# Early-fusion block on one core: attention written out, image outputs around the last softmax, slot maps shared by DVE and ACT

## What is computed

```python
x  = tokens(img, txt)                       # patch embedding, two layer norms, positions
x  = x + scan_mixer(layernorm(x))           # layer 0, a selective scan of 16 states
x  = x + moe0(x)                            # 4 groups x 2 experts of 512, one group per token
q, k, v = norm(x) @ Wq.T, norm(x) @ Wk.T, norm(x) @ Wv.T     # layer 1, q and k with rotary positions
x  = x + softmax(causal(q @ k.T / 16)) @ v @ Wf.T + bf
lg = layernorm(x) @ wr + br                 # 4 experts of 1024, the best two per token
for e in top2(lg): x += gate[e] * (gelu(norm(x) @ w1[e] + b1[e]) @ w2[e] + b2[e])
```

## Time and profile before

| | |
|---|---|
| median of 3 runs | 855.33 us (855.31 to 856.13) |
| profiled execution | 856.54 us, of which the span of instructions is 854.7 us |
| mean granted TensorE clock | 0.935 |
| busy in the span | PE 756.7 us, DVE 507.6, ACT 357.6, POOL 354.1 |
| first product of the layer-0 experts | 146.5 us |
| end of ACT's normalising before them | 133.9 us |
| attention batches | about 378 to 520.8 us |
| image outputs, statistics | to 542.7 us |
| logits, gates, positions | to 559.1 us |
| slot map, first gathers | to 585.0 us |
| layer-1 experts | to 839 us, output to 854.7 |

### The profile page before, as it was taken

The page is one execution under the profiler, slowest core; times in us unless marked ns, Lnnn a source line. Parts: engine busy times, 40 slices in busy tenths (PEclk is TensorE's granted clock), DMA queues, the critical chain, the costliest instruction groups (busy, mean ns, idle before and its releaser), DMA issues.

```text
span 854.7 us, 17322 instructions
## 1 busy us (share of the span) xinstructions
PE 756.7 (89%) x5428; PEld 592.4 (69%) x5429; DVE 507.6 (59%) x1265; ACT 357.6 (42%) x803; POOL 354.1 (41%) x308
## 2 busy tenths in 40 slices
PE   3998932999999999959999999967999999999991
PEld 2767921666666666647777776755888888888871
DVE  4896989433333343349887877795555555555550
ACT  5795663333333333324534333503433334443440
POOL 2449951123232232214556653002455555555431
PEclk9996975999999999969999997987999999999996
DMA  9950044142112121152121210521133333333234
GB/s 264 415 232 2 1 136 155 19 107 33 28 25 37 25 34 27 16 155 90 51 74 50 71 52 29 185 85 51 33 49 49 50 49 49 49 49 49 32 40 139
DMA packets 37174, 65.98 MB, mean 77 GB/s; under 512 B 3776, under 2 KB 29360, under 8 KB 35568
## 3 DMA queue, kind: packets, MB, share of 16 engines
q1 hardware_dynamic: 23696, 46.90, 16.3%
q0 software_dynamic: 13248, 18.21, 13.4%
q10 hardware_dynamic: 192, 0.38, 0.1%
HBM read 44.83 MB, written 23.35 MB: 80 GB/s over the span
## 4 chain that ended last, share of the span: by engine, by line
PE 75%; DVE 15%; ACT 4%; DMA 2%; issue 2%; POOLq 0%; SPq 0%; POOL 0%; DVEq 0%
PE PS L762 15%; PE PS L955 14%; PE PS L968 14%; PE PS L780 7%; PE PS L1299 5%; PE PS L770 2%; PE PS L1340 2%; PE PS L1295 2%; PE PS L1330 2%; PE PS L1332 2%; DVE tops L709 2%; PE PS L1312 1%; PE PS L1303 1%; DMA Y<-in_wtok_dram 1%; PE PS L940 1%
## 5 line engine op out<-in xcount | busy, mean ns | idle before, releaser
L762 PE MATMUL PS<-X,Y 128*128 x576 | 134.7, 384 | 1.3 <-DVE Y L860 1.3
L1125 POOL DMA_INDIRECT sum<-X,dest x45 | 88.4, 1965 | 97.2 <-ACT X L1036 81.9
L968 PE MATMUL PS<-X 128*128 x720 | 125.8, 273 | 1.9 <-ACT X L1036 1.9
L955 PE MATMUL PS<-X 128*128 128x256 f16 (+1 forms) x768 | 124.7, 268 | 2.2 <-DVE X L1056 1.5
L1026 ACT ACTIVATE X<-PS,X 128x256 f32<-128x256 f32 (+1 forms) x192 | 72.8, 463 | 105.8 <-PE PS L955 102.6
L871 DVE SCALAR_TENSOR_TENSOR Y<-PS,Y 128x512 f32<-128x512 f32 x48 | 36.0, 751 | 112.2 <-PE PS L762 112.2
L955 PE MATMUL PS<-X,Y 128*128 128x256 f16 (+1 forms) x384 | 101.1, 267 | 0.0
L926 POOL DMA_INDIRECT sum<-Y,dest x24 | 38.1, 1586 | 148.2 <-ACT Y L837 148.2
L762 PEld LDWEIGHTS PS<-X,Y 128*128 128x128 f16 x576 | 57.0, 99 | 60.8 <-issue 4.3
L968 PE MATMUL PS<-Y,X 128*128 x360 | 98.2, 273 | 0.0
L955 PEld LDWEIGHTS PS<-X 128*128 x768 | 72.3, 98 | 12.8 <-issue 3.0
(11 more groups left out here) (378 smaller groups left out, 1475.8 us busy)
## 6 DMA issues: line engine op xcount, KB each, us to landing
X<-in_w_dram SPq DMA_DIRECT2D x11, 1024.0 KB, 16.1
stage<-in_w_dram SPq DMA_DIRECT2D x16, 512.0 KB, 3.3
sum<-h SPq DMA_DIRECT2D x2, 2048.0 KB, 7.6
xs<-Y SPq DMA_DIRECT2D x2, 1040.0 KB, 5.1
xs<-Y SPq DMA_DIRECT2D x2, 1032.0 KB, 5.5
h<-in_txt_dram SPq DMA_DIRECT2D x2, 1024.0 KB, 17.9
Y<-in_patches_dram SPq DMA_DIRECT2D x3, 672.0 KB, 8.8
sum<-h SPq DMA_DIRECT2D x2, 768.0 KB, 4.0
```

The costliest lines, as they stand in the source:

```text
L762: ins = nc.tensor.matmul(PS[:, 2 * u + s, 0:F0], x_[:, slot, k, :], w_[:, at_:at_ + F0], start=(n == 0), stop=(n == 3 * KC - 1))
L955: ins = nc.tensor.matmul(PS[:, 2 * s + c // 2, (c % 2) * T1:(c % 2) * T1 + tokens], part[:, off:off + P], x_[:, slot, k, 0:tokens], start= ...
L968: ins = nc.tensor.matmul(PS[:, 4 + a, 0:D], h_[:, s, c, a * P:(a + 1) * P], part[:, off:off + D], start=(s == 0 and c == 0 and n == 0), st ...
L1125: nc.gpsimd.indirect_dma_start(out=sum1, out_offset=bass.IndirectOffsetOnAxis(ap=dest[:, i:i + 1], axis=0), in_=y1buf[:, u % 2, i - first_ ...
```

## The change

- All 16 batches are written out on PE, ACT and DVE. `IMAGE_BIAS` = 8 lets the image biases on GpSimd start in batch 8 instead of 6.
- `base_images` goes. Behind the text output of batches 4 to 9 PE makes the base of one image tile in the same bank; DVE scales it in `add_text`. Std (`newt`) is made once at the end of batch 3.
- In batch 15 PE makes image outputs 0, 1 and 2 instead of `base_images`, then transposes, text output 14, values 15, image output 3, text output 15, image outputs 4 and 5. The banks are now 0, 1, 2, 7, 3, 4. DVE adds in a matching order; moments of 14 text tiles are in between.
- Maxima of layer-1 weights are taken in halves of 1,024 (`top_of_half`) in batches 4, 5, 6, 7, 10, 11 and 14, the eighth between the logits and the gates.
- In `positions` the comparisons read integers directly; `minus` is the negated row number; ACT makes the first 6 (layer 0) or 12 (layer 1) token columns of `inrow` as relu(1 - |iota - row|), DVE the others in two or three pieces. Four operations for `source` become one; constants for this (`slot_at`, a repeated `k_tile`) are made on GpSimd at the start.
- The bias products of experts 0 and 1 start once image tile 0 is added. ACT copies both banks of `biases_out` away. The sum is made in parts: experts 0 and 1 and b2 before the slot map, expert 2 behind it, expert 3 behind the transposes of unit 0 (`meanwhile`). The subtraction for `rest1` moves into DVE's unit 0.

```diff
+ACT_ROWS = (6, 12)
+PIECES = (2, 3)
...
+        def act_rows(act, done, inrow):
+            act.wait_ge(rows_known, done + 1)
+            n = ACT_ROWS[done]
+            column = minus.rearrange("p c t -> p (c t)")
+            for c in range(n):
+                nc.scalar.activation(nearly[:, c, :], k_iota, ACT.Abs, bias=column[:, c:c + 1]).then_inc(act_hot, 1)
+            act.wait_ge(act_hot, sum(ACT_ROWS[0:done + 1]) + done)
+            nc.scalar.activation(inrow[:, 0:n, :], nearly[:, 0:n, :], ACT.Relu, bias=1.0, scale=-1.0).then_inc(act_hot, 1)
...
             chain.link(nc.vector.tensor_copy(pos[:, 0:choices, :], slots_of))
-            chain.link(nc.vector.tensor_scalar(low7[:, 0:choices, :], pos[:, 0:choices, :], P - 1, None, ALU.bitwise_and))
-            chain.link(nc.vector.tensor_scalar(high7[:, 0:choices, :], pos[:, 0:choices, :], 7, None,
-                                               ALU.logical_shift_right))
+            chain.link(nc.vector.tensor_scalar(row_of, pos[:, 0:choices, :], P - 1, None, ALU.bitwise_and))
+            nc.vector.tensor_scalar(minus[:, 0:choices, :], row_of, -1.0, None, ALU.mult).then_inc(rows_known, 1)
+            chain.link(nc.vector.tensor_scalar(first_of, pos[:, 0:choices, :], -P, None, ALU.bitwise_and))
-            chain.link(nc.vector.tensor_copy(slots_of, high7[:, 0:choices, :]))
...
-            chain.link(nc.vector.tensor_copy(slots_of, low7[:, 0:choices, :]))
...
-            half = n // 2
-            for c0 in (0, half):
-                nc.vector.tensor_tensor(inrow[:, c0:c0 + half, :], each(slots_of, P)[:, c0:c0 + half],
-                                        along(k_iota, P)[:, c0:c0 + half], ALU.is_equal).then_inc(hot_ready, 1)
+            for c0, c1 in row_pieces(done):
+                nc.vector.tensor_tensor(inrow[:, c0:c1, :], each(row_of, P)[:, c0:c1],
+                                        along(k_iota, P)[:, c0:c1], ALU.is_equal).then_inc(hot_ready, 1)
...
             chain.link(nc.vector.tensor_copy(from_, row_))
-            chain.link(nc.vector.scalar_tensor_tensor(out=place, in0=tile_, scalar=float(P), in1=from_, op0=ALU.mult,
+            nc.vector.scalar_tensor_tensor(out=source[:, 0:tiles], in0=tile_, scalar=float(P), in1=from_, op0=ALU.mult,
+                                           op1=ALU.add).then_inc(source_ready, 1)
+            dve.wait_ge(source_ready, done + 1)
+            chain.link(nc.vector.scalar_tensor_tensor(out=from_, in0=tile_, scalar=float(P), in1=from_, op0=ALU.mult,
                                                       op1=ALU.add))
-            chain.link(nc.vector.tensor_scalar(from_, place, float(TOKENS), -float(TOKENS), ALU.is_ge, ALU.mult))
-            chain.link(nc.vector.tensor_tensor(from_, from_, place, ALU.add))
-            nc.vector.tensor_copy(source[:, 0:tiles], from_).then_inc(source_ready, 1)
-            dve.wait_ge(source_ready, done + 1)
...
             def out_text(b, slot):
...
+                if b in IMAGE_BASE:
+                    n = IMAGE_BASE.index(b)
+                    pe.wait_ge(xTi_copied, n + 1)
+                    for k in range(KC):
+                        ins = nc.tensor.matmul(PS[0:IROWS, 6, PAY1:PAY1 + E1], xTi[:, k, n * IROWS:(n + 1) * IROWS], wr1[:, k, :],
+                                               start=(k == 0), stop=(k == KC - 1))
...
             def batch(b, slot):
                 scores(b, slot)
-                if not known(b, BATCH - 1):
+                if b < BATCH - 1:
                     project(b + 1, 1 - slot)
                 else:
-                    base_images()
+                    pe.wait_ge(v_copied, BATCH)
+                    for n in range(3):
+                        out_image(n)
                 transpose_p(b, slot)
...
             heads(pe, batch)
+            out_image(3)
             out_text(BATCH - 1, 1)
...
+            pe.wait_ge(s_max, BATCH)
+            out_image(4)
+            out_image(5)
...
-            for b in range(START):
+            for b in range(BATCH - 1):
                 batch(b, b % 2)
...
+            maxima(BATCH - 1)
+            normalise_p(BATCH - 1, 1)
+            add_image(0)
+            add_image(1)
+            add_text(BATCH - 2, 0)
+            logit_base()
+            add_image(2)
+            dve.wait_ge(stats_ready, NT + BATCH - 2)
+            moments_text(range(BATCH - 2))
+            add_image(3)
             add_text(BATCH - 1, 1)
-            dve.wait_ge(stats_ready, NT + BATCH)
-            for t in range(BATCH):
-                ins = nc.vector.bn_aggr(mv[:, t, :], stats[:, t, 0, :])
+            add_image(4)
+            add_image(5)
...
-            pe.wait_ge(h3_added, NT)
             biases_out(2)
             pe_count(pe, 1)
-            biases_sum()
+            biases_sum(0, True, False)
+            biases_sum(1, False, False)
+            biases_rest()
             pe_slots(pe, 1, TOPK * NT, SLOT1, inrow1, intile1)
+            biases_sum(2, False, False)
             pe.wait_ge(slots_ready, 2)
             pe.wait_ge(dest_ready, 2)
-            pe.wait_ge(rest_ready, 1)
             pe_scale(pe, 1)
-            pe_experts1(pe)
+            pe.wait_ge(c_copied, 1)
+
+            def meanwhile():
+                biases_sum(3, False, True).then_inc(c_psum, 1)
+            pe_experts1(pe, meanwhile)
```

More of the change, by code:

```diff
@@ L533, in pe_count, with row_pieces @@
                 .then_inc(count_psum, 1)
+        def row_pieces(done):
+            first, last = ACT_ROWS[done], (1 + done) * NT
+            step = -(-(last - first) // PIECES[done])
+            return [(c, min(c + step, last)) for c in range(first, last, step)]
+        def act_rows(act, done, inrow):
[6 more added lines that the diff above has]
+            nc.scalar.activation(inrow[:, 0:n, :], nearly[:, 0:n, :], ACT.Relu, bias=1.0, scale=-1.0).then_inc(act_hot, 1)
         def pe_slots(pe, done, n, tiles, inrow, intile):
+            pieces = [c for c, _ in row_pieces(done)]
+            earlier = done * len(row_pieces(0))
+            pe.wait_ge(act_hot, sum(ACT_ROWS[0:done + 1]) + done + 1)
+            pe.wait_ge(hot_ready, earlier + 1)
             for i in range(n):
-                if i % (n // 2) == 0:
-                    pe.wait_ge(hot_ready, 2 * done + i // (n // 2) + 1)
+                if i in pieces:
+                    pe.wait_ge(hot_ready, earlier + pieces.index(i) + 1)
                 ins = nc.tensor.matmul(PS[:, 7, 0:3 * tiles], inrow[:, i, :], intile[:, i, :, :].rearrange("p a b -> p (a b)"),
@@ L724, in dve_scale @@
             top, scale_, un = amax[:, 2:3], hscale[:, 2 * layer:2 * layer + 1], hscale[:, 2 * layer + 1:2 * layer + 2]
-            chain.link(nc.vector.tensor_reduce(top, PS[:, 5 + layer, 0:P], AX, ALU.max))
+            chain.link(nc.vector.tensor_reduce(top, PS[:, 5 - layer, 0:P], AX, ALU.max))
             if layer == 0:
@@ L981, in tile @@
                     transpose_x(0, 0, 0)
+                    meanwhile()
                 products_in(i, 0, w_, slot)
@@ L1473, in run @@
                 chunk(b, slot, j)
-            for b in range(START):
+            for b in range(BATCH):
                 run(b, b % 2, b // 2)
-            with act.Fori(START // 2, BATCH // 2 - 1) as j:
-                run(2 * j, 0, j)
-                run(2 * j + 1, 1, j)
-            run(BATCH - 2, 0, BATCH // 2 - 1)
-            run(BATCH - 1, 1, BATCH // 2 - 1)
         def pool_attention(pool):
@@ L1657, in logit_base, with add_image @@
                 chain.link(nc.vector.tensor_tensor(raw1, raw1, old, ALU.add))
-            for b in range(START):
-                batch(b, b % 2)
-            with dve.Fori(START // 2, BATCH // 2 - 1) as j:
-                chain.begin(j - START // 2, 4)
-                batch(2 * j, 0)
-                batch(2 * j + 1, 1)
-                chain.end(BATCH // 2 - 1 - START // 2)
-            batch(BATCH - 2, 0)
-            batch(BATCH - 1, 1)
+            def add_image(n):
+                r = tile_rows(BATCH + n)
+                dve.wait_ge(bi_added, n + 1)
+                dve.wait_ge(pr_psum, PR_IMAGE[n])
+                hb = h[0:r, BATCH + n, :]
+                to = raw1[0:r, :, BATCH + n:BATCH + n + 1]
+                nc.vector.tensor_tensor(to, PS[0:r, OUT_BANK[n], D:PAY1].unsqueeze(2), to, ALU.add)
+                nc.vector.tensor_tensor(hb, PS[0:r, OUT_BANK[n], 0:D], hb, ALU.add).then_inc(h3_added, 1)
+                dve.wait_ge(h3_added, H3_IMAGE[n])
+                nc.vector.bn_stats(stats[:, BATCH + n, 0, :], h[:, BATCH + n, :]).then_inc(stats_ready, 1)
@@ L1732, in biases_out, with biases_sum @@
                 ins.then_inc(c_psum, 1)
-            def biases_sum():
+            def biases_sum(e, first, last):
+                for c in range(F1 // P):
+                    off = e * W1N + KC * F1 + c * D
+                    for n, (g_, w_) in enumerate(((gbh, w1h), (gbh, w1l), (gbl, w1h))):
```

(14 more changed lines are left out.)

187 lines of the change are left out of this document (92 added, 95 removed).

## The result

The kernel after takes 840.48 us, the median of 4 runs (838.78 to 841.64), against 855.32 for the kernel before (853.39 to 856.13, 4 runs): ratio 0.9828, 95% interval 0.9803 to 0.9853, or 14.8 us less. The forecast was 841.0. The profiled execution took 838.78 us (span 836.9) against 856.54 (span 854.7) before.

What follows compares the result with a forecast made beforehand. PE was taken as nearly gapless except after the last scores (21.89 us) and before layer 1's experts (25.93), both at clock 0.69. Terms 2.5 - 8.8 + 0.2 - 1.6 - 7.1 + 0.3 = -14.5 gave 840.8, say 841.0 us; range 838.0 to 846.5.

Steps and rivals of the forecast that it cites:

- Step 1: Attention batches: the loop's back edge costs PE nothing, so writing it out is worth 0.
- Step 2: Batches 4 to 9: small image-base matmuls lengthen each by 0.42 us, +2.5 in all; half reduces on DVE cost 0.
- The slower rival: Attention batches: small matmuls drop the clock in six batches; six falls would give about 882 us; chance 0.04.
- Step 3: Last scores to variance: 21.9 us becomes 13.1, -8.8, if the clock stays at 2.4 GHz; DVE ends it.
- Step 4: Variance to slot arithmetic: same operations plus the last half reduce in DVE's wait for ACT's exponential, +0.2 us.
- Step 5: Slot map of layer 0: fewer rows on DVE, casts and linked operations gone; first products 1.6 us earlier.
- ACT is late: Slot map of layer 0: ACT's Abs and Relu need table loads, map 2.4 us later, 843.4 us; chance 0.06.
- Step 6: Slot map of layer 1: map ready 2.0 us earlier, source numbers 2.6, destinations 2.4; integer operands cost nothing.
- Step 7: Behind layer 1's map: rest product and maxima reduces leave the path, expert 3's biases join it; first expert products, -7.1 us.
- low clock before the experts: Before layer 1's experts: transposes and expert 3's biases wholly or partly at half speed, +1.6 to +3.7 us; chance 0.24.
- The rest product: Layer-1 experts: the rest product now stands ahead of the first split of h, +0.3 us.

Runs made afterwards that it cites:

- unroll_only: The kernel before with its attention loop of 16 batches written out on PE, ACT and DVE, nothing else changed: 854.65 us, ratio 0.9984.
- slot_maps_only: The kernel before with only the slot map part of the change (rows shared with ACT, integer comparisons, short source, merged semaphores): 849.05 us, ratio 0.9934.
- the kernel with the gap filled: The kernel after with expert 3's biases ahead of the first tile's transposes, in the wait for the gather: 838.40 us, run again 839.02 us.
- outputs_behind_wait: The kernel after with image outputs 0 to 2 behind the transposes of batch 15 instead of ahead of them: 843.28 us, ratio 0.9856.
- fill_both_pauses: The kernel after with expert 3's biases in the gather wait and expert 2's biases ahead of the slot products: 838.83 us, ratio 0.9822.

## Why the prediction was right, and where it was not

The time came out within the range and 0.5 us from the forecast, and the large steps hold. But one term was too large and a part outside the sum made up for it, by luck, so the total is better than its parts.

- **Step 1, the loop: 0.** Right: unroll_only has the same 132.64 us from first to last scores. "Runtime: NRT & Kernel Launch" in the Trainium skill, section "Instruction fetch mechanics", warns that a taken branch stalls the fetch where its target isn't in the two pages of instructions at hand. The trace shows no such cost here: 8.79 us per batch with the back edge and without it.
- **Step 2, small matmuls in the batches: +2.5.** Measured +2.1: each of the six batches is 0.36 longer, not 0.42, and the clock stays at 1.00 in them. Two neighbouring batches of the kernel after, from one start of scores to the next, the first with a base:

```profile
471.83:480.98 9.15, 9.15 (x59) 7.21 (x58) 6.96 (x23) 3.33 (x11) 5.58 (x6) 1.00 0.19 57
480.98:489.77 8.79, 8.79 (x55) 6.82 (x54) 7.38 (x23) 3.33 (x11) 5.46 (x6) 1.00 0.22 62
```

  PE is full in both. The half reduces on DVE lengthen no batch: 11 has one and no base and keeps 8.79, as 12 and 13 do, and of the batches with a base, 10 has one and 8 and 9 have none, at 9.15 all three. The slower rival, six falls of the clock, did not occur. It was worth its chance all the same: the same matmuls, 24 in a row, did lower the clock once.
- **Step 3, the end of attention: -8.8.** Measured -8.8 (21.89 to 13.11), step by step as worked out: DVE ends it, PE's last image outputs are done 10.1 us after the last scores (10.8 forecast), the variance comes at 13.1. Its condition, that the clock stays up without the block and the wait, was the right one: both cost when put back.
- **Step 4: +0.2.** Measured +0.1. The half reduce took 1.21 us and lies almost wholly in the wait for the exponential.
- **Step 5, the map of layer 0: -1.6.** Measured -1.7 in the kernel after and in slot_maps_only alike. ACT made its rows without a table load and in time, so "ACT is late" did not occur: PE's first product of the map waited for ACT's Relu, which ended at 133.73, but its last ended at 135.43, before DVE took the result at 135.54. The rule of "ScalarE: Activation LUTs" in the Trainium skill, section "Rules for kernel authors", that I weighed there is to use VectorE for relu. With all but one row in each layer left to DVE the time was 842.7 us instead of 840.5 (act_rows_1): it is a rule about the rate of one engine, and here the other is the path.
- **Step 6, the map of layer 1.** Source 12.58 us after the row number by starts, against 15.12: -2.5, forecast -2.6. Integer operands cost nothing in the big comparisons: 4,096 elements in 4.55 us are 1.11 ns each, against 6.08 for 5,632, 1.08, with float operands.
- **Step 7, what stood behind the map: -7.1.** Here the forecast failed by 1.8. The order of events is as told: bound off the path, gather next (landed at 564.26, 17.8 after the row number; 17.7 forecast), transposes, biases of expert 3, products. The step that failed is "24 matmuls, 2.63 at 2.4 GHz": they took 4.29, and the transposes 0.66. That is the rival *low clock before the experts*, given 0.24 and 1.6 to 3.7 us. I had called the pause 1.5 us; it was 2.71. My own figures (map at 571.3, 2.63 of biases, first tile at 576.8) give 2.9 with the biases at full clock, so the pause was mis-sized in my own numbers. The pause ended at full clock, and I had taken the clock at the end of a pause as what counts; it is the microseconds behind it that were slow. The two executions of the kernel after both show it, and the kernel with the gap filled shows it gone in one and moved in the other.
- **The rest product: +0.3.** From the end of the first block on, the two executions differ by +0.2; nothing in the runs tells this from chance.
- **Outside the sum: -1.5** between layer 0's first product and the first scores, a stretch to which I had given no term; in it the clock rose earlier and lay higher (slot_maps_only), for a reason that stays open. It hides that step 7 fell short: -15.0 behind the start is -14.5 + 1.8 (step 7) - 0.4 (step 2) - 0.1 (step 4) - 0.1 (step 5) - 0.1 (rest) and -1.5, and rounding. Had this stretch not moved, the sum would have been some 842 on the scale of the median, still in the range.

## What to carry to other kernels

Look for short stretches between stages where PE has little to do, and price them at both clock levels: here two of them, under 50 us of 855, held most of the gain, and much of it was PE work that kept 2.4 GHz rather than work removed. Put work that is ready into the pause itself and not behind it (image outputs ahead of the transposes; biases ahead of the tile's transposes, at best 838.4 us), and then look for the next pause, since the clock can fall there instead. When you move work off an engine's path, find what is late next before you count it: 4.6 us of reduces behind the map were worth 3.0, because 2.3 of them lay beside a wait for the gather.

## What the runs showed of the hardware that I had not expected

- The granted clock can fall late: in the kernel after it reads 1.00 through a pause of 2.71 us and 0.50 from 565, when PE has been at work again for 0.7 us; in outputs_behind_wait a pause of 3.04 us ended at 523.12 and 0.50 came from 524. In fill_both_pauses PE stood for 4.14 us before 555.2, the clock was 1.00 in all of it and 0.52 from 556 to 557. It isn't always late: in the kernel after PE's longer pause before the slot products begins at 547.00, and the clock reads 0.50 from 548.
- The same instructions can keep the clock in one execution and lose it in another: 24 small matmuls took 2.50 us at 1.00 and 3.36 with a fall inside, with no idle time just ahead of them or in them in either.
- The early part of these kernels moves by up to 3.7 us between executions (125.39 to 129.12 at the same mark), while the 15 batches of the three kernels with the old attention take 132.64 us to the hundredth. A difference of a few microseconds is safer read from marks than from spans.
